# Attention and a mixture of experts: the first block's experts start when two of its four tiles are ready

## The reference

```
x = x + attn(layernorm(x)) ; x = x + ffn(layernorm(x))
attn: q, k, v = split(x @ w_qkv); 16 heads of 16; rope on q and k; q, k = elu(. * SCALE) + 1
      kv += k (x) v ; ks += k            (running sums over the tokens before and at t)
      out_t = (q . kv) / max(q . ks, 1e-6) ; out @ w_out
ffn:  w = routing weights of 8 experts (sigmoid(x @ Wr / temperature), zone test, exp; top-2 fallback)
      out = sum over e of w[e] * ((silu(x @ Wg[e]) * (x @ Wu[e])) @ Wd[e])     every expert for every token
```

## Time and profile before

| | |
|---|---|
| median of three runs | 802.93 us |
| the profiled execution | 803.36 us, of which the span from first to last instruction is 801.4 us |
| PE busy | 758.3 us (95%) |
| DVE, ACT, POOL busy | 607.1, 465.7, 482.6 us |
| mean granted TensorE clock | 0.974 of 2.4 GHz |
| chain that ended last | PE 87%, DVE 6% |

### The profile page before, as it was taken

One profiled execution on the slowest core, in us unless ns is written; L12 is line 12 of the kernel. 1 busy time (PEld: TensorE's weight loads), 2 busy tenths in 40 slices (PEclk: granted clock), 3 DMA queues, 4 the chain that ended last, 5 costly groups with the idle time before them and its releaser, 6 DMA issues.

```text
span 801.4 us, 18061 instructions
## 1 busy us (share of the span) xinstructions
PE 758.3 (95%) x6660; PEld 650.4 (81%) x6660; DVE 607.1 (76%) x1597; ACT 465.7 (58%) x886; POOL 482.6 (60%) x537
## 2 busy tenths in 40 slices
PE   5475899999999999999999999999999999999998
PEld 3364688888888888888888888888888888888887
DVE  6788797879877797778877697877977788756344
ACT  3664766666566665666665566566556665634222
POOL 3686678765666666556667565665665656653322
PEclk9766999999999999999999999999999999999999
DMA  4644134122110222121111321110211121100000
GB/s 140 128 95 108 47 85 94 40 43 68 41 28 15 43 66 41 41 43 47 35 28 40 43 67 40 41 35 10 66 42 40 40 54 28 28 1 27 1 1 27
DMA packets 97319, 38.27 MB, mean 48 GB/s; under 512 B 74192, under 2 KB 96976, under 8 KB 97232
## 3 DMA queue, kind: packets, MB, share of 16 engines
q1 hardware_dynamic: 90704, 30.83, 17.7%
q10 hardware_dynamic: 6528, 6.29, 2.7%
HBM read 16.13 MB, written 4.19 MB: 25 GB/s over the span
## 4 chain that ended last, share of the span: by engine, by line
PE 87%; DVE 6%; ACT 2%; issue 2%; POOL 2%; DMA 1%; SPq 0%; DVEq 0%; ACTq 0%; POOLq 0%
PE y L475 21%; PE gate L441 21%; PE up L441 21%; PE front L301 6%; PE front L302 3%; PE back L353 3%; PE back L397 3%; PE up L372 2%; PE up L409 1%; PE front L324 1%; PE front L422 1%; PE back L341 1%; PE back L384 1%; POOL a_lo L1188 1%; DVE am L839 1%
## 5 line engine op out<-in xcount | busy, mean ns | idle before, releaser
L1217 POOL TENSOR_TENSOR h_lo<-work,h_hi 128x512 fp32r<-128x512 f32 x126 | 163.1, 1295 | 59.4 <-ACT h_hi L677 59.4
L1188 POOL TENSOR_TENSOR a_lo<-am,a_hi 128x512 f16<-128x512 f32 x120 | 144.3, 1204 | 54.0 <-ACT a_hi L604 51.2
L475 PE MATMUL y<-wd_hi,h_hi 128*128 128x256 f32 x504 | 145.9, 289 | 0.0
L475 PE MATMUL y<-wd_lo,h_hi 128*128 128x256 f32 x504 | 140.5, 279 | 0.0
L1061 DVE TENSOR_TENSOR work<-work,up 128x512 f32<-128x512 f32 x128 | 87.0, 680 | 70.3 <-PE up L441 70.0
L475 PE MATMUL y<-wd_hi,h_lo 128*128 128x256 f32 x504 | 140.2, 278 | 0.0
L1077 DVE SCALAR_TENSOR_TENSOR xa<-y,wo,xa 128x256 f32<-128x256 f32 x252 | 111.9, 471 | 1.9 <-PE y L475 1.9
L677 ACT ACTIVATE h_hi<-work 128x512 fp32r<-128x512 f32 x126 | 79.3, 630 | 58.3 <-DVE work L1061 36.4
L475 PEld LDWEIGHTS y<-wd_hi,h_hi 128*128 128x128 f32 x504 | 94.8, 188 | 4.1
L475 PEld LDWEIGHTS y<-wd_lo,h_hi 128*128 128x128 f32 x504 | 95.0, 188 | 2.8
L604 ACT ACTIVATE a_hi<-am 128x512 f16<-128x512 f32 x120 | 74.9, 625 | 35.2 <-DVE am L839 35.2
(11 more groups left out here) (220 smaller groups left out, 1741.5 us busy)
## 6 DMA issues: line engine op xcount, KB each, us to landing
xr<-xT SPq DMA_DIRECT2D x32, 128.0 KB, 2.6
xa<-x SPq DMA_DIRECT2D x32, 128.0 KB, 2.6
out<-xa SPq DMA_DIRECT2D x32, 128.0 KB, 1.7
xa<-Wg ACTq DMA_DIRECT2D x8, 256.0 KB, 3.1
work<-Wd ACTq DMA_DIRECT2D x8, 256.0 KB, 3.0
work<-Wu ACTq DMA_DIRECT2D x8, 256.0 KB, 2.9
work<-w_qkv SPq DMA_DIRECT2D x2, 384.0 KB, 3.7
qT<-q_st SPq DMA_TRANSPOSE x32, 3.2
```

Source lines behind the costliest of these rows:

```text
L475: m = pe.matmul(y_bank(n, t), h_at(hi, n)[:, t * P:(t + 1) * P], wd_p[wi][:, u // KI, u % KI, :], start=(n % KI == 0 and (t % 2 == 0 or n ...
L1188: pool.tensor_tensor(a_p[1][:, heads(r), :], am_place(g, r).rearrange("p (h n) -> p h n", h=4), a_p[0][:, heads(r), :], ALU.subtract).then ...
L1217: pool.tensor_tensor(h_at(1, n), hb[:, n % 2, :], h_at(0, n).bitcast(F32), ALU.subtract).then_inc(s_hlo, 1)
```

## The change

It does five things at once.

1. **Block 0 in three parts.** `GROUPS` splits the routing of block 0 in two (tiles 0 and 1, tiles 2 and 3), and its 16 units become: n = 0 to 3, experts 0 to 3 whole (both halves) on tiles 0 and 1; n = 4 to 11, experts 4 to 7 on all four tiles, as before; n = 12 to 15, experts 0 to 3 whole on tiles 2 and 3. The eight units on two tiles ("pairs") have twelve products of 256 columns each in `gate` and in `up` where a unit has six of 512.
2. **Order.** Every engine's list is written out up to step 9 in place of step 4; from step 10 (n = 20) the loop is the old one. `gate(0)` now stands behind x2_T of tile 1.
3. **Banks.** Only tiles 0 and 1 use the experts' banks; `state` uses a back bank up to tile 8.
4. **Raw weights in place.** Each weight matrix is loaded by SP into the memory of its own low part, and the low part overwrites it; the ring and its waits go, and ACT issues no DMA. The high part's copy waits for all three matrices of its expert.
5. **Cosine.** `tcos_scale` (1/std times the cosine table, 8 numbers wide, on DVE) goes; `cos` multiplies by 1/std, as a scalar from memory, and by the table in one instruction.

```diff
+HF = 2
+PAIR = HF * P
+SPLIT = 4
+GROUPS = ((0, 0, 2), (0, 2, 2)) + tuple((b, 0, NT) for b in range(1, NB))
+X2_AHEAD = {2: 2, 3: 4, 4: 7, 5: 10, 6: 12, 7: 15}
+S0 = 9
...
+        def halved(n):
+            return n < SPLIT or UNITS - SPLIT <= n < UNITS
+        def expert(n):
+            if n >= UNITS:
+                return n % UNITS // KI
+            return n if n < SPLIT else (n + SPLIT) // KI if n < UNITS - SPLIT else n - UNITS + SPLIT
+        def tiles_of(n):
+            return HF if n < SPLIT else NT * (n // UNITS + 1)
...
+            def three_pair(ps, weights, n):
+                for m_ in range(KI):
+                    q = 0
+                    for wi, xi in ((0, 0), (1, 0), (0, 1)):
+                        for k in range(KD):
+                            m = pe.matmul(ps[:, m_ * PAIR:(m_ + 1) * PAIR], weights[wi][:, expert(n), k, m_ * P:(m_ + 1) * P],
+                                          x2[xi][:, 0, k, unit_tokens(n)], ...)
...
             def gate(n):
-                w.wait_ge(*slab_lo_done(3 * (u // KI)))
-                w.wait_ge(s_x2lo, NT * (b + 1))
+                w.wait_ge(*slab_lo_done(3 * expert(n)))
+                w.wait_ge(s_x2lo, tiles_of(n))
                 w.wait_ge(s_g, n)
...
-            for s in range(LAG, STEPS):
+            for s in range(10, STEPS):
...
             def slab_hi(n):
-                w.wait_ge(slab_in[n % NSL], 16 * (n // NSL + 1))
-                act.activation(dst[0][:, e_, :, :], ring[n % NSL], ACT.Copy).then_inc(s_slab_hi, 1)
-                load_slab(n + NSL - 1)
+                _, raw, dst, e_ = slabs[n]
+                w.wait_ge(expert_in[e_], 48)
+                act.activation(dst[0][:, e_, :, :], raw[:, e_, :, :], ACT.Copy).then_inc(s_slab_hi, 1)
...
-            def tcos_scale(g):
-                v.tensor_scalar(tcos[:, :], tabs[:, g // NT % 2, g % NT, 0:HALF], rstd1[:, g % NRS:g % NRS + 1], None, ALU.mult).then_inc(s_tcos, 1)
...
             def cos(g):
-                v.tensor_tensor(qk_bank(g)[:, :].rearrange("p (h d) -> p h d", d=HALF),
-                                qk_bank(g)[:, :].rearrange("p (h d) -> p h d", d=HALF), bcast(tcos[:, :], 1, 4 * H),
-                                ALU.mult).then_inc(s_cos, 1)
+                qk_r = qk_bank(g)[:, :].rearrange("p (h d) -> p h d", d=HALF)
+                v.scalar_tensor_tensor(out=qk_r, in0=qk_r, scalar=rstd1[:, g % NRS:g % NRS + 1],
+                                       in1=bcast(tabs[:, g // NT % 2, g % NT, 0:HALF], 1, 4 * H), op0=ALU.mult,
+                                       op1=ALU.mult).then_inc(s_cos, 1)
...
-            setup_first()
-            for g in range(NT):
-                rstd1_pow(g)
-            sin(0, 1); sin(0, 0); slab_lo(0); v_rest(0); sin(1, 1); sin(1, 0); v3(0); slab_lo(1); v_rest(1)
+            setup_first(); slab_lo(0); slab_lo(1); rstd1_pow(0); rstd1_pow(1); rstd1_pow(2); sin(0, 1); sin(0, 0)
+            slab_lo(3); slab_lo(4); sin(1, 1); sin(1, 0); slab_lo(6); v_rest(0); slab_lo(7); slab_lo(9); v3(0)
```

More of the change, by code:

```diff
@@ L143, in build @@
         sb("h_gap", [P, 8])
[L144 to L145 removed]
+        hb = sb("hb", [P, 2, B])
         h_p = [sb(f"h_{s}", [P, 2, B], F32R) for s in ("hi", "lo")]
@@ L233, in h_at, with x2T_ahead, routers_before @@
+        def units_ahead(g):
+            return X2_AHEAD[g] if g in X2_AHEAD else min(NT * (g - NT) + 3, NB * UNITS)
+        def x2T_ahead(n):
+            return sum(1 for g in range(NTL) if early(g) or units_ahead(g) <= n)
+        def routers_before(g):
+            return sum(1 for j in range(1, NG) if last_tile(j) + 1 < g)
         def h_at(part, n):
@@ L242, in live, with live_group @@
             return 0 <= g < NTL
-        def tiles(g):
-            return min(g + 1, NTL)
+        def live_group(j):
+            return 0 <= j < NG
         def live_unit(n):
             return 0 <= n < UNITS * NB
-        slabs = [(src, dst, e_) for e_ in range(E) for src, dst in ((Wg, wg_p), (Wu, wu_p), (Wd, wd_p))]
-        ring = [xa[:, 10:12, :]] + [stage[:, i, :].rearrange("p (k n) -> p k n", k=KD) for i in range(2)]
-        def slab(s, i):
-            if s < LAG:
-                n = 3 * s + i
-                return n if i < 3 and n < HEAD_SLABS else None
-            n = HEAD_SLABS + STEP_SLABS * (s - LAG) + i
-            return n if i < STEP_SLABS and n < SLABS else None
+        slabs = [(src, raw, dst, e_) for e_ in range(E)
+                 for src, raw, dst in ((Wg, wg_raw, wg_p), (Wu, wu_raw, wu_p), (Wd, wd_raw, wd_p))]
         def slab_lo_done(n):
@@ L1100, in vector_program @@
-            for s in range(LAG, STEPS):
+                b = n // UNITS
+                if halved(n):
+                    at, y = t + (0 if n < SPLIT else HF), Y[n % 2][:, t * D:(t + 1) * D]
+                    w.wait_ge(s_down, n + 1)
+                    w.wait_ge(s_acc, 2 * n + t - 1)
+                else:
+                    at, y = t, y_bank(n, t)
+                    w.wait_ge(*((s_last, t + 1) if n == LAST + 2 else (s_down, n // KI * KI + KI)))
+                    w.wait_ge(s_acc, 2 * n + t - (1 if n == SPLIT and t < HF else 3))
@@ new lines, in vector_program @@
+            acc(3, 1); mask(5, 2); ln2(4); var_eps(10); mask(5, 3); cos(6); rope(6); acc(4, 0); x2_lo(4); phi(6)
+            o_sum(5, 0); o_sum(5, 1); den_max(5); route_ix2(1); den_rec(5); k_lo(6); norm(5); q_lo(6); route_s2(1)
+            h_up(7); o_lo(5); acc(4, 1); route_both(1); st_add(5); route_out(1); x1_add(5); x_lo(7); acc(4, 2)
+            acc(4, 3); mask(6, 0); mask(6, 1); bn2(5); h_up(8); acc(6, 0); mask(6, 2); mask(6, 3); mean_var2(5)
+            acc(6, 1); acc(6, 2); var_eps2(5); h_up(9); cos(7); acc(6, 3); rope(7); o_sum(6, 0); o_sum(6, 1); phi(7)
@@ new lines, in vector_program @@
+            ln2(7); x2_lo(7); mask(8, 0); mask(8, 1); acc(12, 0); acc(12, 1); h_up(15); mask(8, 2); mask(8, 3)
+            acc(13, 0); x_lo(9); route_sum(2); route_zone(2); acc(13, 1); h_up(16); o_sum(8, 0); o_sum(8, 1)
+            route_nearest(2); den_max(8); acc(14, 0); acc(14, 1); den_rec(8); route_weight(2); norm(8); cos(9)
+            acc(15, 0); acc(15, 1); rope(9); o_lo(8); h_up(17); phi(9); x_lo(10); x1_add(8); bn2(8); mean_var2(8)
+            k_lo(9); q_lo(9); var_eps2(8); route_first(2); h_up(18); ln2(8); route_second(2); route_tie(2)
```

611 lines of the change are left out of this document (341 added, 270 removed).

## The result

The changed kernel takes 807.26 us in the median (806.02 to 808.09), the kernel before 802.76 in the same session: a ratio of 1.0052 (95% interval 1.0036 to 1.0068), 0.5% slower. A fourth run of the changed kernel took 1876.11 us, for a reason that no trace shows; it counts in the median of 807.26 (806.43 without it), but neither in the range in brackets nor in the ratio. The forecast was 798.5, the range 789 to 808. The profiled execution took 806.43 us (span 804.7).

What follows compares the result with a forecast made beforehand. PE was taken to bound the kernel, busy 95% of the span. First gate 65.5 + 124.6 work + 7 loss puts unit 20 at 197.1, not 200.9 (-3.8); with -0.6 behind it, -4.4 us: median 798.5, range 789 to 808.

Steps and rivals of the forecast that it cites:

- Tile 0's scores at 29: Head of the kernel: tile 0's scores start at 29 us, 27.03 before; sign range 28 to 31.
- The first gate at 65.5: End of the head: the experts' first product starts at 65.5 us (61 to 70), 83.92 before.
- DVE's work between the first gate and unit 20: Block 0: DVE's work grows from 98.0 to 120.3 us, with two more tiles and one more routing.
- The cosine's cost at nothing: Cosine on DVE: taking its scalar from memory costs 0 to 0.06 us a tile, counted as nothing.
- the removed tcos at 0.6 us: Loop behind unit 20: 22 tcos fall away; of PE's 1.1 us idle up to 790, 0.6 come back.
- rival D: ACT up to 200 us: six more table loads of 1.28 us on PE's path, 7.7 in all, 806; chance 0.05.
- one of its own signs of being wrong: First gate to unit 20: the prediction is wrong if DVE is below 86% busy and PE waits for it all the same.
- PE's loss between the two gates: First gate to unit 20's gate: PE loses 7 us, three more than now; ends 4.0 and 14.
- PE's own work: First gate to unit 20: 113.0 us dense, plus 10.1 attention, 0.9 routing and 0.6 pairs, sum 124.6.
- B: Block 0: DVE becomes the bound, not busy above 84%; unit 20 at 205.5, total 806.9 (up to 811); chance 0.19.
- A: Block 0 denser: first gate at 63, losses of 4, unit 20 at 191.6, total 793.0 (down to 788); chance 0.16.
- C: Block 0, gains cancel: first gate at 68, losses of 8, unit 20 at 200.6, total 802.0; chance 0.18.

Runs made afterwards that it cites:

- cos_only: The kernel before with only the cosine edit: table scalings gone, the cosine product takes 1/std as a scalar from memory; 802.08 us, ratio 0.9991 to the kernel before.
- pool_late: The changed kernel with GpSimd's splits of three expert matrices moved later, out of the routing of tiles 0 and 1; 806.63 us, ratio 1.0042 to the kernel before.
- after_long_dve: The changed kernel with an unused statistics instruction on DVE behind each of block 0's 32 sums; 810.89 us, ratio 1.0100 to the kernel before.
- before_long_dve: The kernel before with an unused statistics instruction on DVE behind each of block 0's 32 sums; 808.26 us, ratio 1.0083 to the kernel before.

## Why the prediction was wrong

**Right.** Tile 0's scores at 29 (28.26). The first gate at 65.5 (64.45 here; from 62.8 to 66.3 in the variants). DVE's work between the first gate and unit 20, 120.3 us (119.07). The cosine's cost at nothing and the removed tcos at 0.6 us: cos_only gained 0.6. That table loads stand beside other work (rival D). And one of its own signs of being wrong was met, narrowly: DVE is busy for 119.07 of 138.55 us, 85.9%, below 86, and PE waits for it all the same.

**The step that failed** is PE's loss between the two gates: "So PE's loss must grow. Ends: 4.0, as now, and 14 ... I take 7". It is 10.5 us of idle and 1.3 at the low clock (PE is busy 28.44 us up to gate 4 in the changed kernel and 27.15 for the same work in pool_late, at full clock), 11.8. Two things were wrong with the step. First, it didn't follow from its own figures: for units 0 to 3 the prediction has some 30 us of DVE beside 25 of PE, which is 5 us of waiting in that stretch alone, and 5.3 came; with 7 for the whole it left 2 at most for gate 4 to 20, where 5.2 came. Second, it went by DVE's mean share, and the share doesn't give the size: from gate 4 to 20 DVE is busy for 84% in both kernels, and PE idles 5.20 us in one and 0.69 in the other. What PE waits for there are single results that its list needs earlier than they come. The upper end was also summed wrongly: 120.3 us of DVE in 124.6 + 14 are 87%, and 84% is reached only with a loss of 18.6; and the 134 us behind the "90%" are not the 131.6 of the forecast (91%). The row of the kernel before that stood for its room, 84% with 4.0 us of loss, was read as more room than there was: 9.4 us of DVE added to it cost 6.0.

**Smaller terms.** PE's own work was sized 124.6 and is 128.02 less 1.3, 126.7. From gate 4 to 20 it is 99.58 against 92.35 before, 7.2 for one tile's attention (6.1 by the working) and four pairs (0.3); where the rest comes from no run shows. With the first gate 1.05 us early, these make 197.1 - 1.05 + 2.1 + 4.8 = 203.0, unit 20's gate as found. Behind it I gave back 0.6 and it cost 1.2: 0.9 of it stand between gates 20 and 24, where the timeline of PE has one wait more, and every form with the new order has 23.5 us or more there and every form with the old one 22.6 to 22.7.
```profile
210.16 0.76 PE L429 MATMUL up<-vx,k_st 128*128 128x34 bf16 x24 [0.65 <-DVE hb L1147]
```

**The rivals.** B gave the number, 806.9, by luck, and names the engine of most waits; its mechanism, a ceiling at 84%, is refuted by 90% in after_long_dve and 87% in before_long_dve, and its unit 20 stood at 205.5, not at 203.0. A and C needed losses of 4 and 8 us. So the change does what it says, starts PE's work 19.5 us earlier, moves 14 us of PE's work (128.0 busy for 114.0: two tiles, a routing, the pairs) and 21 us of DVE's (119.1 for 97.9) behind the first gate, and 7.5 us more of idle time eat the remaining 5.4 and 2.1 besides.

**Shown and not shown.** Shown: the loss belongs to the three-part block 0 and what came with it, and not to the cosine or the weights in place; it stands as 7.5 us more idle time of PE between the gates, mostly waits for DVE, and 2.1 us more work than sized; added DVE work turns into the same kind of idle time in the kernel before; less DVE time ahead of gate 4 takes idle time away, most where GpSimd held an instruction ahead of a wait of PE; waits moved within PE's list come back. Not shown: what makes most of the 10.5 us, since 7 us less of DVE left 9.0 of them; whether the waits for the transposes, 3.3 us, come from the DMA or from what feeds it; that DVE's time alone makes all of the 5.3 us up to gate 4, since no run cut more than 2.2 us there; and what part a better list, written for these latencies as a whole, could win back.
